# A two-part graph network in fp32: quads of 512 nodes laid out four nodes to a partition, degrees counted two quads ahead, and the GCN bias added by VectorE in PSUM

## What is computed

```python
deg = segment_sum(ones, dst, n)            # own loop counted
dinv = rsqrt(deg)
norm = dinv[src] * dinv[dst]
def layer(h, W, b):
    h = h @ W.T
    msg = h[src] * norm[:, None]
    agg = segment_sum(msg, dst, n)
    return relu(agg + b)
h = layer(x, W1, b1); h = layer(h, W2, b2); h = layer(h, W3, b3)
```

## Time and profile before

| | |
|---|---|
| runs, us | 3917.22, 3922.1, 3923.7 (median 3922.1) |
| the profiled execution | 3924.44 us, of which the span of its trace 3922.7 us |
| granted TensorE clock, mean | 0.93 of 2.4 GHz |
| PE, DVE, ACT, POOL busy | 89%, 75%, 64%, 61% of the span |

### The profile page before, as it was taken

The page is one execution under the profiler, slowest core; times in us unless marked ns, Lnnn a source line. Parts: engine busy times, 40 slices in busy tenths (PEclk is TensorE's granted clock), DMA queues, the critical chain, the costliest instruction groups (busy, mean ns, idle before and its releaser), DMA issues. The chain is left out here.

```text
span 3922.7 us, 95283 instructions
## 1 busy us (share of the span) xinstructions
PE 3489.8 (89%) x27850; PEld 3444.3 (88%) x27850; DVE 2951.4 (75%) x8362; ACT 2512.3 (64%) x5223; POOL 2378.3 (61%) x2466
## 2 busy tenths in 40 slices
PE   4999999999999354447999999799999979999998
PEld 3999999999999344337999999799999979999998
DVE  6888888888887677775666666466666648888887
ACT  1666666666666587873555555355555549999999
POOL 4444444444441566647777777577777757777773
PEclk8999999999999555558999999899999989999998
DMA  4555555555552699986776776567667659999996
GB/s 121 162 156 155 155 155 153 156 156 153 154 156 86 236 347 341 350 311 196 226 227 226 229 226 221 165 227 228 224 228 226 227 189 291 302 301 298 297 298 213
DMA packets 793236, 859.89 MB, mean 219 GB/s; under 512 B 137123, under 2 KB 704566, under 8 KB 793128
## 3 DMA queue, kind: packets, MB, share of 16 engines
q1 hardware_dynamic: 696114, 653.35, 51.8%
q0 software_dynamic: 94080, 205.13, 17.7%
q10 hardware_dynamic: 2934, 0.16, 0.1%
HBM read 652.78 MB, written 257.52 MB: 232 GB/s over the span
## 5 line engine op out<-in xcount | busy, mean ns | idle before, releaser
L471 POOL DMA_INDIRECT rows<-x_in,node_i x490 | 517.0, 1055 | 662.0 <-DVE raw L1042 513.8
L471 POOL DMA_INDIRECT rows<-x_scratch,node_i x490 | 533.7, 1089 | 187.6 <-issue 149.0
L471 POOL DMA_INDIRECT rows<-ga_scratch,node_i x490 | 533.5, 1089 | 177.5 <-issue 177.5
L471 POOL DMA_INDIRECT rows<-gb_scratch,node_i x490 | 503.9, 1028 | 199.5 <-issue 133.6
L1418 DVE TENSOR_TENSOR gcn_agg_lo<-gcn_agg_ps,gcn_agg_hi 128x1024 fp32r<-128x1024 f32 x196 | 240.0, 1224 | 490.2 <-ACT gcn_agg_hi L1441 474.8
L1441 ACT CAST gcn_agg_hi<-gcn_agg_ps 128x1024 fp32r<-128x1024 f32 x196 | 199.2, 1016 | 607.4 <-PE gcn_agg_ps L499 607.4
L499 PE MATMUL gcn_agg_ps<-gcn_select,gcn_rows_hi 128*128 128x256 f32 (+2 forms) x1960 | 554.7, 306 | 13.4 <-DVE gcn_rows_lo L1427 13.4
L499 PE MATMUL gcn_agg_ps<-gcn_select,gcn_rows_lo 128*128 128x256 f32 (+2 forms) x1960 | 535.6, 302 | 0.0
L954 ACT ACTIVATE h1t_hi<-h1t_ps,b_sb 128x256 fp32r<-128x256 f32 x392 | 165.1, 473 | 471.5 <-issue 356.7
L512 PE MATMUL gcn_h_ps<-g_hi,gcn_agg_hi 128*128 128x256 f32 x1568 | 442.8, 282 | 0.0
L512 PE MATMUL gcn_h_ps<-g_hi,gcn_agg_lo 128*128 128x256 f32 x1568 | 442.0, 282 | 0.0
(11 more groups left out here) (196 smaller groups left out, 12457.0 us busy)
## 6 DMA issues: line engine op xcount, KB each, us to landing
own<-x_in SPq DMA_DIRECT2D x196, 256.0 KB, 3.1
h_scratch<-h2t SPq DMA_DIRECT2D x196, 256.0 KB, 2.3
h2t_in<-h_scratch SPq DMA_DIRECT2D x98, 512.0 KB, 5.3
x_sb<-x_in SPq DMA_DIRECT2D x98, 512.0 KB, 7.0
x_scratch<-x SPq DMA_DIRECT2D x98, 512.0 KB, 5.5
gcn_own<-x_scratch SPq DMA_DIRECT2D x98, 512.0 KB
ga_scratch<-gcn_h SPq DMA_DIRECT2D x98, 512.0 KB, 3.4
gcn_own<-ga_scratch SPq DMA_DIRECT2D x98, 512.0 KB
```

The lines of the kernel that those rows point to most:

```text
L471: pool.indirect_dma_start(out=c["rows"][:, slot, b], out_offset=None, in_=source[:, :], in_offset=bass.IndirectOffsetOnAxis(ap=c["node"][: ...
```

## The change

1. `quad_rows` lays a quad out with four neighbouring nodes to a partition, so a load or store has one run of 4 KB in each partition. Tile `j` is now the nodes `4 n + j`. The selection matrix is written tile by tile, its numbers read from `iota32` with a step of 4; `agg_ps` takes it in four pieces (`by_tile`), and is then already in the order of tiles. In `norm_pass` `tile_columns` reads `zt` with a step of 4. The degree's split of a node number is changed to match.
2. In `norm_pass` all work but the counting moves two steps back (SP from 0 and 6 to 2 and 8, ACT from 1, 4, 5 to 3, 6, 7, PE's `z_ps` from 2 to 4, DVE from 3 and 5 to 5 and 7). `degree` on DVE moves from lag 5 to 6. The count, its read-out and ACT's `root` stay.
3. In the first two GCN passes the bias matmul, the `root_row` load and its waits are gone. DVE does four `scalar_tensor_tensor` on `h_ps` in place, first in its step at lag 5, and ACT waits for them (`biased`) in place of `dense_done`. `last_pass` keeps its bias matmuls. The bias rows are loaded to all partitions in `constants`, whose tiles `layer_b...` shrink from 768 to 256 columns.

```diff
--- before.py
+++ after.py
+PART = P // 4
...
-        layer_b = m.sb("layer_b", [3, 3 * D])
+        layer_b = m.sb("layer_b", [3, D])
...
-                for k, name in enumerate(("gb1", "gb2", "gb3")):
-                    act.dma_start(layer_b[:, k * D:(k + 1) * D], dram[name].rearrange("(o d) -> o d", o=1)
+                for name in ("gb3",):
+                    act.dma_start(layer_b[:], dram[name].rearrange("(o d) -> o d", o=1)
                                   .broadcast_to([3, D])).then_inc(c["rows_in"], 16)
-                for name in ("b_edge",):
+                for name in ("b_edge", "gb1", "gb2"):
                     act.dma_start(c[name][:], dram[name].rearrange("(o d) -> o d", o=1)
                                   .broadcast_to([P, D])).then_inc(c["rows_in"], 16)
...
 def quad_rows(dram, q):
 
-    return dram[bass.ds(q * QUAD, QUAD), :].rearrange("(j p) d -> p j d", p=P)
+    return dram[bass.ds(q * QUAD, QUAD), :].rearrange("(p j) d -> p j d", j=4)
 
 
 def tile_columns(cols, j):
 
-    return cols[:, j * P:(j + 1) * P]
+    return cols.rearrange("p (n j) -> p j n", j=4)[:, j]
+
+
+def by_tile(cols):
+
+    return cols.rearrange("p (j n) -> p j n", j=4)
 
 
 def select_columns(nc, c, quad, select):
 
     for b, (first, end) in enumerate(SPAN):
-        last = nc.vector.tensor_scalar(select[:, b, 0:(end - first) * P], c["iota32"][:, first * P:end * P],
+        last = nc.vector.tensor_scalar(by_tile(select[:, b, 0:(end - first) * P]),
+                                       c["iota32"][:, first * P:end * P].rearrange("p (n j) -> p j n", j=4),
                                        c["place"][:, bass.ds(quad.q, 1), b], None, ALU.is_equal)
     return last
...
     for h in range(2):
         for j in range(4):
-            nc.tensor.matmul(tile_columns(out[:, h], j), own[:, s, j, h * P:(h + 1) * P], c["ident"][:],
+            nc.tensor.matmul(out[:, h, j * P:(j + 1) * P], own[:, s, j, h * P:(h + 1) * P], c["ident"][:],
                              start=j == 0, stop=False, is_transpose=True, skip_group_check=True)
     pe.wait_ge(rows_split, quad.done())
     pe.wait_ge(select_done, quad.done())
     for k, (first, end) in enumerate(SPAN):
         for h in range(2):
             for rows in (rows_hi, rows_lo):
-                last = nc.tensor.matmul(out[:, h, first * P:end * P], rows[:, b, k, h * P:(h + 1) * P],
-                                        select[:, b, k, 0:(end - first) * P], start=False,
-                                        stop=k == BLOCKS - 1 and rows is rows_lo, skip_group_check=True)
+                last = nc.tensor.matmul(by_tile(out[:, h])[:, :, first * PART:end * PART],
+                                        rows[:, b, k, h * P:(h + 1) * P], by_tile(select[:, b, k, 0:(end - first) * P]),
+                                        start=False, stop=k == BLOCKS - 1 and rows is rows_lo, skip_group_check=True)
     return last
 
-def dense_nodes(nc, c, quad, out, parts, weight, layer):
+def dense_nodes(nc, c, quad, out, parts, weight, bias_row=None):
 
     for j in range(4):
-        nc.tensor.matmul(out[:, j], c["root_row"][:, quad.slot, j * P:(j + 1) * P], c["bias_row"][:, layer],
-                         start=True, stop=False)
+        if bias_row is not None:
+            nc.tensor.matmul(out[:, j], c["root_row"][:, quad.slot, j * P:(j + 1) * P], bias_row[:],
+                             start=True, stop=False)
         terms = [(h, a, w) for h in range(2) for a, w in products(parts, weight)]
         for n, (h, a, w) in enumerate(terms):
-            last = nc.tensor.matmul(out[:, j], tile_columns(a[:, h], j), w[:, h],
-                                    start=False, stop=n == len(terms) - 1)
+            last = nc.tensor.matmul(out[:, j], a[:, h, j * P:(j + 1) * P], w[:, h],
+                                    start=n == 0 and bias_row is None, stop=n == len(terms) - 1)
     return last
...
-                    if quad := at(0):
+                    if quad := at(2):
...
-                    if quad := at(6):
+                    if quad := at(8):
                         sp.wait_ge(x1_ready, quad.done())
...
-                    if quad := at(1):
+                    if quad := at(3):
                         b, s = quad.b, quad.slot
...
-                    if quad := at(4):
+                    if quad := at(6):
                         b = quad.b
...
                             .then_inc(sd_ready, 1)
-                    if quad := at(5):
+                    if quad := at(7):
...
-                    if quad := at(2):
+                    if quad := at(4):
                         b = quad.b
...
-                nc.vector.tensor_scalar(low_i[:], place_i[:], P - 1, None, ALU.bitwise_and).then_inc(split_done, 1)
+                nc.vector.tensor_scalar(low_i[:], place_i[:], 2, None, ALU.arith_shift_right).then_inc(split_done, 1)
-                nc.vector.tensor_scalar(tile_i[:], place_i[:], 7, None, ALU.arith_shift_right).then_inc(split_done, 1)
+                nc.vector.tensor_scalar(tile_i[:], place_i[:], 3, None, ALU.bitwise_and).then_inc(split_done, 1)
...
                 def step(at):
-                    if (quad := at(5)) and quad.place == 0:
+                    if (quad := at(6)) and quad.place == 0:
                         degree(quad)
-                    if quad := at(5):
+                    if quad := at(7):
                         b = quad.b
...
-                    if quad := at(3):
+                    if quad := at(5):
                         b, s = quad.b, quad.slot
...
-                    if quad := at(5):
+                    if quad := at(7):
...
-                    if quad := at(1):
-                        if quad.has(QUAD_RING):
-                            sp.wait_ge(dense_done, quad.before(QUAD_RING))
-                        load_root_rows(sp, c, dram, quad, loaded[quad.slot])
                     if quad := at(6):
                         sp.wait_ge(h_ready, quad.done())
                         sp.dma_start(quad_rows(target, quad.q), h[:, quad.slot]).then_inc(stored[quad.slot], 16)
...
-                        dense_nodes(nc, c, quad, h_ps[:, b], [agg_hi[:, b], agg_lo[:, b]], weight, layer)\
+                        dense_nodes(nc, c, quad, h_ps[:, b], [agg_hi[:, b], agg_lo[:, b]], weight)\
                             .then_inc(dense_done, 1)
                     if quad := at(2):
...
-                        pe.wait_ge(loaded[quad.slot], quad.landed(2))
+                        pe.wait_ge(loaded[quad.slot], quad.landed(1))
...
                 def step(at):
+                    if quad := at(5):
+                        b = quad.b
+                        dve.wait_ge(dense_done, quad.done())
+                        for j in range(4):
+                            last = nc.vector.scalar_tensor_tensor(out=h_ps[:, b, j], in0=bias[:],
+                                                                  scalar=c["root"][:, quad.tile(j)], in1=h_ps[:, b, j],
+                                                                  op0=ALU.mult, op1=ALU.add)
+                        last.then_inc(biased, 1)
                     if quad := at(3):
...
                     if quad := at(5):
                         s = quad.slot
-                        act.wait_ge(dense_done, quad.done())
+                        act.wait_ge(biased, quad.done())
```

More of the change, by code:

```diff
@@ L1340, in _, with gcn_pass @@
                 quad_pipeline(dve, step)
[L1341 removed]
+                dve.wait_ge(row_steps, 2)
                 nc.vector.tensor_tensor(row_lo[0:parts], row_ps[0:parts], row_hi[0:parts].bitcast(F32), ALU.subtract)\
[L1343 to L1346 removed]
+                    .then_inc(row_steps, 1)
+def gcn_pass(nc, keep, dram, name, source, target, bias, weight):
     c = keep
@@ L1458, in _, with last_pass @@
                 quad_pipeline(act, step)
-def last_pass(nc, keep, dram, source, layer, weight):
+def last_pass(nc, keep, dram, source, weight):
     c = keep
@@ L1530, in step @@
                             pe.wait_ge(res_added, quad.before(2))
-                        dense_nodes(nc, c, quad, h_ps[:, b], [agg_hi[:, b], agg_lo[:, b]], weight, layer)\
+                        dense_nodes(nc, c, quad, h_ps[:, b], [agg_hi[:, b], agg_lo[:, b]], weight, c["bias_row"])\
                             .then_inc(dense_done, 1)
```

48 lines of the change are left out of this document (23 added, 25 removed).

## The result

The changed kernel takes 4067.9 us (median of 4 runs, 4066.5 to 4076.4) against 3922.1: ratio 1.0378, interval 1.0366 to 1.039. It is slower by 146 us; the forecast was 3879 us. The profiled execution took 4068.1 us with a span of 4066.4. Nine of the eighteen runs of the experiments fell where the kernel before took 4587 to 4714 us at a granted clock of about 0.89 instead of 0.93; they are marked "at the low clock", nothing is argued from their times, and the expectations put this down to the chip, though the record has chip numbers 1 and 13 beside both kinds.

A forecast was written before the change was run, and what follows sets the result against it. PE and POOL were taken to bound the GCN passes, ACT the last pass, DMA partly `norm_pass`. GCN -43, last pass 0, `norm_pass` 0 from 3924.4 gave 3881, the median 2.3 lower: 3879 us, range 3835 to 3935.

The forecast's parts named there:

- PE and POOL are level: GCN passes: PE's period of 6.97 us a quad equals POOL's 6.98, so taking work from PE exposes POOL.
- POOL's new period of 6.75 us: GCN passes: POOL sets the pace at the mean of 6.61, 6.66 and 6.98 us a quad, gaining 43 us.
- its price on DVE: GCN passes: four bias additions start 0.40 us apart, adding 1.6 us a quad, at most 1.9.
- All this is nothing while DVE's sum stays below the period: GCN passes: the additions' new waits are covered, costing nothing while DVE's work a quad is below the period.
- the pricing of the strided read: Selection in GCN passes: reading in steps of 4 costs DVE 0.37 us a quad, between 0 and 0.80.
- The first rival: GCN passes: strided read costs DVE 0.80 us or more a quad, DVE becomes the bound, 3909 us; chance 0.20.
- factor 1.46: Selection: cost per column of a strided read, taken from PE weight loads, 2.63 against 1.80 ns.
- R2: GCN passes: additions and selection at their high prices, DVE's work 7.1 us, period 7.13, 3962 us; chance 0.14.
- R4: GCN passes: `rows_lo` keeps meeting gathers, POOL stays at 6.98 us, 3922 us or slower by some; chance 0.14.
- Last pass: Last pass: DVE's 6.67 us a quad stays below ACT's 7.05, so the change is nothing.
- R1: The first rival, chance 0.20: GCN passes -23 us, last pass +5 with DVE at 7.1 us a quad, `norm_pass` +5.
- `norm_pass`: right at 0: `norm_pass`: read-outs 18.0 us apart gain 6 us, a later start costs 6; sum 0, between -15 and +15.

The follow-up runs named there:

- part 3 alone: Kernel before with only the bias moved from PE matmuls to DVE additions in the first two GCN passes, old layout, read and lags: 3917.2 us against 3918.3.
- the contiguous read: Changed kernel, all three parts, with the selection reading a table already in the order of tiles instead of in steps of 4: 3893.9 us against 3918.3.
- the additions spread out: DVE's additions moved between the `rows_lo` instructions, contiguous read: 3885.3 us from the changed kernel, 3884.1 in the old layout without parts 1 and 2.
- Layout and lags alone: Changed kernel with a contiguous selection read and the bias by matmuls again: 3920.7 us against 3922.2, ratio 0.9999.

## Why the prediction was wrong

**PE and POOL are level: right, but POOL's new period of 6.75 us was not.** "Taking work from PE exposes POOL" is what the table shows. But the 6.75 was the mean of three rows, and the forecast gave no reason why the gathers should be held less once PE had less to do. With part 3 alone POOL needs 5 x (1.084 + 0.305) = 6.95 us and, in the second pass, 7.04: next to and beyond the upper end of 6.98 (the sum's range up to 3905 had used 6.9), and the forecast gain of 43 us was 1. With all parts and the contiguous read it is 5 x (1.065 + 0.305) = 6.85 and 24 us. Only with the additions spread out, an edit the forecast did not have, is it 6.76 to 6.80. One reading under that term was also wrong: most gathers that meet `rows_lo` do not pass undisturbed. Of the 237 that start in it in the kernel before, 166 took over 1.15 us.

**Part 3: right in its price on DVE.** The additions start (1.66 - 0.48)/3 = 0.39 us apart, forecast 0.40, in the row at 2105.63. DVE's busy time in the GCN pass is 629.9/98 = 6.43 us a quad, forecast 6.39. But the sentence "All this is nothing while DVE's sum stays below the period" was wrong: it asks whether DVE has the time, and not what POOL can do in it. With the strided read in place the additions cost 106 us (4068 against 3962).

**Part 1: here the prediction failed.** The step is the pricing of the strided read: it was counted as time of DVE alone, and its price on POOL was put at nothing. For DVE the size came out nearly right. These are the groups by shape, 1850 to 3100 us, of the kernel before, of the changed kernel, and of the changed kernel with the contiguous read:

```profile
L482 DVE TENSOR_SCALAR gcn_select<-iota,place 128x384 fp32r<-128x384 f32 x350 | 145.9, 458 | 0.0
L482 DVE TENSOR_SCALAR gcn_select<-iota,place 128x256 fp32r<-128x256 f32 x350 | 125.0, 357 | 10.7 <-PEq L636 10.7
L482 DVE TENSOR_SCALAR gcn_select<-iota,place 128x128 fp32r<-128x128 f32 x175 | 48.8, 279 | 0.0
```

```profile
L488 DVE TENSOR_SCALAR gcn_select<-iota,place 128x384 fp32r<-128x384 f32 x316 | 167.7, 576 | 0.0
L488 DVE TENSOR_SCALAR gcn_select<-iota,place 128x256 fp32r<-128x256 f32 x316 | 143.5, 454 | 6.3 <-PEq L644 6.3
L488 DVE TENSOR_SCALAR gcn_select<-iota,place 128x128 fp32r<-128x128 f32 x158 | 53.5, 339 | 0.0
```

```profile
L489 DVE TENSOR_SCALAR gcn_select<-iota_tile,place 128x384 fp32r<-128x384 f32 x356 | 134.6, 419 | 0.0
L489 DVE TENSOR_SCALAR gcn_select<-iota_tile,place 128x256 fp32r<-128x256 f32 x356 | 125.1, 351 | 6.3 <-PEq L645 6.3
L489 DVE TENSOR_SCALAR gcn_select<-iota_tile,place 128x128 fp32r<-128x128 f32 x178 | 54.6, 307 | 0.0
```

The selection of a quad takes 2 x 0.576 + 2 x 0.454 + 0.339 = 2.40 us by records, 2.03 by the run of five, where that run was 1.61: +0.42, forecast 0.37. The first rival's +0.80 did not come. The Trainium skill's rule in "Advanced Engine Details and Errata", section "SBUF Cachelines", which I had made that rival of, points the right way; the page names no size for the penalty, and the doubling was mine. From 128 to 384 columns the trace has 0.93 ns a column with the step of 4, against 0.70 in the kernel before. Against the same instruction with only the read made contiguous, 0.44, it is double; that instruction is no shorter in all (1.85 us by records, before 1.91), since it starts from a higher base.

That 0.37 came so near was luck. Its factor 1.46 set a weight load where the granted clock is 1.00 (`found`, window from 20 to 35 us) against one of another width where it is 0.56. The same load with and without the step, both in a stretch at 1.00 (1360.0 to 1363.2 us before, 1411.5 to 1414.6 us in the changed kernel), happens to give the same factor, 208/142; over the whole pass, most of it at the lower clock level, the medians are 226 and, before, 230 ns.

```profile
L1237 PEld LDWEIGHTS z_ps<-ident,zt 128*128 128x128 f32 x8 | 0.9, 142 | 1.8 <-DVE res L1303 1.8
```

```profile
L1245 PEld LDWEIGHTS z_ps<-ident,zt 128*128 128x128 f32 x5 | 0.7, 208 | 2.0 <-ACT zt L1200 2.0
```

What the sum lacked is a term for POOL. I held the port question for settled by the kind of operation (two SBUF inputs, `rows_lo`) and looked only at how DVE's new work adds up. The price of the read was 0.42 us on DVE, which is covered, and 5 x (1.236 - 1.089) = 0.74 us on POOL with the additions ahead of it, which isn't: 0.74 x 196 = 145 us. The Trainium skill, "SBUF — State Buffer", section "SBUF: two separate sides", also names modes of DVE, besides two inputs, in which the port pair is taken; the trace of the kernel before shows a selection that let 230 of 231 gathers pass, and the changed kernel one that doesn't. What decides it is the step of the read, since the run with the contiguous read changes nothing else; by what mechanism the step does it, no run here shows.

R2, the slower rival, had the right place and the wrong mechanism: it wanted DVE's work above 6.97 us a quad. It was 6.43, and the kernel lost anyway, 106 us more than R2 gave. The tail of R4 ("held more still, slower by some us") had the mechanism, with a size of "some us" that I had not worked out: no row of the kernel before could have given it, since its selection let gathers pass.

**Last pass: right in its period.** `fin_y` comes every 7.06 us, forecast 7.05. The pass is 5 us longer all the same (its gathers 1.111 against 1.028). That is the number of R1's +5 and not its reason, since DVE's work is 663.9/98 = 6.77 us a quad, below 7.05. From its first gather the pass takes 733 to 735 us in the three kernels that read in steps of 4 there, and 728 to 729 in the eight that don't.

```profile
3699.92 2.14 ACT L1657 ACTIVATE fin_y<-fin_res,fin_shift,fin_rs 128x256 f32<-128x256 f32 x4
3706.98 2.14 ACT L1657 ACTIVATE fin_y<-fin_res,fin_shift,fin_rs 128x256 f32<-128x256 f32 x4
```

**`norm_pass`: right at 0.** The read-outs come (1747.8 - 1314.4)/24 = 18.06 us apart, forecast 18.0, the first transposes start 3.6 us later (1317.1 against 1313.5), forecast 6, and the DMA share in its middle fell from 1.00 to 0.96 at 348 GB/s against 347.

```profile
L1345 DVE TENSOR_TENSOR degree<-deg_ps,hist_from_one x25: 141/175/175, 1314.4 to 1747.8; 128x16 f32 x21, 128x16 f32<-128x16 f32 x4
1340.00:1740.00 400.00, 190.47 (x1134) 165.40 (x1134) 314.44 (x1312) 325.07 (x641) 248.85 (x429) 0.58 0.96 348
```

Layout and lags alone take 3921 us, so the two together are worth nothing; no run separates them, and a gain of one could hide a loss of the other.

## What to carry to other kernels

When two engines are level and a change moves work off one, price the change on the other one too, and not only in time spent: ask of each edited instruction whether the second engine could run beside it before and still can. The mean duration of the second engine's instructions, sorted by what the first was doing at their start, answers that in one table. An instruction whose access pattern changes is a new instruction for this purpose, even if its engine has time for its longer duration; here a table of numbers stored in the right order costs 2 KB a partition and is worth 174 us.

## What was not expected of the hardware

- A DVE selection with one SBUF input let gathers pass when it read contiguously (1.02 us in the mean) and held them when it read fp32 in steps of 4 (1.20 to 1.72).
- How long a gather was held went, in part, with how long DVE had been running without a pause: 1.2 to 1.4 us after 1 to 3 us of running, 1.9 to 2.0 after 4 to 6, but 1.4 to 1.5 after more. Why is open; so is whether the pause is the cause.
- Of the 166 gathers that start in `rows_lo` and are held in the kernel before, 106 end 0.87 us after its last instruction and most others inside it. With an addition that reads PSUM between every two of them, a gather that started in `rows_lo` took 1.11 us in the mean.
- A PE weight load of 128 columns with a step of 4 took 208 ns against 142 at the upper clock level, but over the whole of `norm_pass`, mostly at the lower level, the medians were 226 and 230.
